# VectorE's order at the group ends and in the drain of a fused convolution and quantised MLP

## The chip, the cores and the metric

One core of a Trainium2 chip runs the whole program. The metric is the time of one execution on the device, in microseconds (us).

## The reference

The input x is 16 images of 192 channels and 32 x 32 pixels, in float32. Two residual blocks follow one another:

```
x = x + dwconv7x7(layernorm_over_channels(x), symmetrised weights)
t = tokens(x)                                   # 16 x 1024 tokens of 192
h = q(layernorm(t) @ sign(W1 - mean).T + b1)    # 768 wide
h = gelu(h, exact)
t = t + q(h @ sign(W2 - mean).T + b2)           # 192 wide
# q, for each of 5 groups of 3 images: gamma = max|y| over the group,
#   clip(y * 128 / (gamma + 1e-5), -128 + 1e-5, 128 - 1e-5); image 16 gives 0
```

The point that shapes the schedule is q: no GELU of a group of images can be computed before the largest absolute value of the group's whole first product is known, and no output before that of the second product.

## The kernel before, in words

Up to about 240 us the program transposes and normalises x, makes the band matrices and does the convolution on TensorE. The change doesn't touch that part. What follows is the token loop, one Python loop `for s in range(-2, FT + LAGF)` written out separately for each engine. The order of the instructions on an engine is the order of this code, and the engines meet only by semaphores. Nothing is rearranged by a planner.

A unit is half an image, 512 tokens. There are FT = 30 units in five groups of GT = 6. Each unit goes through a pipeline over the steps s:

- step u - 2: VectorE normalises four blocks (`normal`, L816), from step 6 on for unit s + 2.
- step u - 1: TensorE turns the tokens round (`tokens`, L1008, L1011), ScalarE and VectorE split them into high and low parts (`token_high`, L546, L548; `token_low`, L822, L824).
- step u: TensorE computes the hidden values in six parts (`hidden`, L1022 to L1024), ScalarE evicts them with the bias (L560).
- step u + 1: VectorE takes the largest absolute value (`largest`, L844). At a group's last unit it also reduces the six values (L847).
- step u + 6 (LAGA): ScalarE's three GELUs (`gelus`, L566). They need the group's scale. In a step with s % 6 == 0 they come at the end of the step.
- step u + 7 (LAGH): the rounding to float16, partly by ScalarE (`high`, L573), partly by VectorE (`high`, L831). Up to unit 22 GpSimd then makes the low parts in six subtractions (L435); from unit 23 (LAST) on VectorE makes half of them itself (L839), GpSimd three.
- step u + 8 (LAG2): TensorE's second product, `lower` (L1054, six pairs of matmuls spread over the step) and `upper` (L1064). The high and low parts lie in two buffers by the unit's parity, so the casts of unit u wait until `upper` of unit u - 2 has ended (`mm2[1]`).
- step u + 9 (LAGE): ScalarE evicts the result (`result`, L584, L587), VectorE takes its largest value (`largest2`, L870, L874).
- step u + 15 (LAGF): the output, `final` (L897, L898): result times scale plus x, where x was turned round by TensorE into two banks of PSUM (`x_back`, L995, L998, L1000) in the step before. TensorE turns x of the next unit into the same banks only when `final` of the last one has ended (`fin`). SyncE stores the output and then fetches x of a later unit from DRAM (`bring_back`), since most of x is parked there.

A group end is a step with s % 6 == 0 from 6 to 30, called `first` in the code. There the scale of the finished group is made: VectorE reduces the six maxima, TensorE transposes them into a row (`as_row`, L1029, on the third part of the step), VectorE reduces the row (`over_row`, L851), TensorE spreads the number to all partitions (`to_all`, L1034, on the fourth part), VectorE computes the scale in five small instructions (`scale`, L856 to L866), and ScalarE's GELUs use it. The row lies in the bank that `final` reads, so TensorE's transpose waits both for the maxima (`gmx`) and for `final` of unit s - 15. TensorE's turning of x on the fifth part of the step waits for the scale. `first2` (s = 15, 21, 27, 33, 39) is the same for the second product (`over_row(1, ..)`, `scale2`).

The drain is the part with s > 30: no hidden products are left, only GELUs (to step 35), casts (to step 36), second products (to step 37) and outputs. The last scale and the last six outputs come in steps 39 to 44.

Of the kernel before, what the change touches and what calls it, by code (L numbers as in the profile page):

```python
# [42 lines left out]
FT = (B // GROUPS * GROUPS) * 2  # L43
# [13 lines left out]
LAGF = LAGE + GT  # L57
# [28 lines left out]
def build(nc, x, cw, w1, b1, w2, b2, out):  # L86
    ctx = ExitStack()
    with ctx:
# [535 lines left out]
        def _(dve):  # L624
# [224 lines left out]
            def over_row(k, g):  # L849
                dve.wait_ge(gtr[k], g)  # L850
                v.tensor_reduce(gs[0:1, k:k + 1], row, AX.X, ALU.max).then_inc(gone[k], 1)  # L851
# [50 lines left out]
            for s in range(-2, FT + LAGF):  # L902
                for k in range(1, len(BATCH)):
                    if BSTEP[k] + 2 == s:
                        scales(k)
                g, g2 = s // GT, (s - LAGF) // GT + 1
                first, first2 = s % GT == 0 and 1 <= g <= FT // GT, (s - LAGF) % GT == 0 and 0 <= s - LAGF < FT
                if first:
                    if 0 <= s - LAGH < FT:
                        high(s - LAGH)  # L910
                    largest(s - 1)
                    if 0 <= s - LAGF < FT:
                        final(s - LAGF)
                    over_row(0, g)
                if s > 5 and s + 2 < FT:
                    normal(s + 2)
                if not first and 0 <= s - LAGH < FT:
                    high(s - LAGH)
                if first2:
                    over_row(1, g2)  # L920
                elif not first and 0 <= s - LAGF < FT:
                    final(s - LAGF)
                if first:
                    scale(g)
                elif 1 <= s <= FT:
                    largest(s - 1)
                if first2:
                    scale2(g2)
                    final(s - LAGF)
                if 0 <= s + 1 < FT:  # L930
                    token_low(s + 1)
                for k in range(len(BATCH)):
                    if BSTEP[k] == s:
                        statistics(k)
                if s == -2:
                    scales(0)
                    normal(0)
                if 0 <= s - LAGE < FT:
                    largest2(s - LAGE)
# [212 lines left out]
```

## Time and profile before

| | |
|---|---|
| median of 3 runs | 635.79 us (635.36 to 638.39) |
| profiled execution, span | 636.4 us |
| TensorE busy | 504.6 us (79%) |
| VectorE busy | 457.2 us (72%) |
| ScalarE busy | 382.7 us (60%) |
| GpSimd busy | 216.1 us (34%) |
| chain that ended last | PE 40%, ACT 23%, DVE 15%, DMA 12%, issue 5% |

The profile comes from one execution of its own, whose span is 0.6 us above the median of the timed runs; no other time is given for it. In the page and the rows PE is TensorE's matmuls, PEld its weight loads, DVE is VectorE, ACT ScalarE, POOL GpSimd, and L844 a line of the kernel. In brackets stands how long the engine was idle before an instruction and what released it. PEclk is the granted clock of TensorE as a share of full speed; its levels are 1.2 and 2.4 GHz. Busy shares are means over stages that have different limits, so each place has to be read for itself.

### The profile page before, as it was taken

What the parts mean: (1) busy time and instruction counts of PE and PEld (TensorE: products, weight loads), DVE (VectorE), ACT (ScalarE), POOL (GpSimd) and SP (SyncE); (2) the same over time, 40 slices, a digit from 0 to 9 for tenths busy, and PEclk for the clock granted to TensorE, in tenths of its full rate; (3) what the DMA queues carried; (4) which work ended last, traced back from release to release, by engine and by line L of the source; (5) the groups of instructions that cost most, each with busy time, mean ns of one, the idle gap of its engine ahead of it and who ended that gap; (6) DMA issues with size and microseconds to landing.
All of it is one profiled execution on the core that took longest, in us unless ns stands there. A gap on an engine that the chain in (4) does not pass through costs nothing.

```text
span 636.4 us, 9847 instructions
## 1 busy us (share of the span) xinstructions
PE 504.6 (79%) x3552; PEld 355.1 (56%) x3552; DVE 457.2 (72%) x1041; ACT 382.7 (60%) x598; POOL 216.1 (34%) x221
## 2 busy tenths in 40 slices
PE   3347348999799987668699899989998999768683
PEld 3346348999799974233345445545564565435452
DVE  7989841222259987977899788897988688665655
ACT  2798920000001355457999799969997798857730
POOL 4000100000300003210486556574848357534430
PEclk9777769999989997789899899989999899979998
DMA  7997225656955639800111001231133333512355
GB/s 221 298 349 205 79 78 165 165 163 172 223 140 142 183 113 396 289 1 1 56 45 51 25 1 41 66 95 49 54 96 101 95 104 100 174 60 90 100 150 173
DMA packets 55280, 81.29 MB, mean 128 GB/s; under 512 B 7361, under 2 KB 39105, under 8 KB 55232
## 3 DMA queue, kind: packets, MB, share of 16 engines
q1 hardware_dynamic: 39616, 68.28, 35.0%
q10 hardware_dynamic: 15136, 11.22, 6.3%
q0 software_dynamic: 480, 1.17, 0.9%
q8 instruction: 28, 0.46, 0.3%
q14 instruction: 20, 0.16, 0.1%
HBM read 53.12 MB, written 27.53 MB: 127 GB/s over the span
## 4 chain that ended last, share of the span: by engine, by line
PE 40%; ACT 23%; DVE 15%; DMA 12%; issue 5%; SPq 3%; ACTq 1%; DVEq 0%
PE bank L972 16%; ACT arena L566 7%; ACT arena L560 6%; DMA arena<-kz_d 5%; PE bank L1054 5%; DMA arena<-x 5%; DVE am L844 5%; PE bank L1064 3%; PE bank L1022 3%; PE bank L1024 2%; PE bank L1023 2%; ACT arena L573 2%; ACT arena L482 2%; PE bank L995 2%; DMA arena<-park_d 2%
## 5 line engine op out<-in xcount | busy, mean ns | idle before, releaser
L435 POOL TENSOR_TENSOR arena<-arena 128x512 f16<-128x512 f32 x159 | 183.2, 1190 | 142.7 <-DVE arena L831 108.6
L560 ACT ACTIVATE arena<-bank,b1s 128x512 f32<-128x512 f32 x180 | 124.7, 703 | 51.7 <-PE bank L1024 51.3
L972 PE MATMUL bank<-arena 128*128 128x112 f32 (+1 forms) x1152 | 135.3, 281 | 21.8 <-ACT arena L482 12.4
L972 PEld LDWEIGHTS bank<-arena 128*128 128x128 f32 x1152 | 133.8, 197 | 22.9 <-ACT arena L482 12.7
L1054 PE MATMUL bank<-arena 128*128 128x512 f16 x360 | 107.7, 394 | 1.7 <-ACT arena L584 1.7
L566 ACT ACTIVATE arena<-arena,gm 128x1024 f32<-128x1024 f32 x90 | 102.7, 1163 | 8.0 <-DVE gm L866 8.0
L844 DVE TENSOR_REDUCE am<-arena 128x1 f32<-128x3072 f32 x30 | 100.3, 3345 | 2.3 <-ACT arena L560 2.3
L750 DVE TENSOR_TENSOR arena<-bank,arena 128x512 f32<-128x512 f32 x48 | 33.2, 692 | 81.2 <-PE bank L972 81.1
L1022 PE MATMUL bank<-arena 128*128 128x512 f16 x180 | 72.0, 400 | 22.6 <-DVE arena L824 11.3
L497 ACT ACTIVATE arena<-arena,wmean 51x576 f16<-51x576 f32 (+1 forms) x10 | 8.6, 856 | 129.2 <-DVE wmean L724 116.4
L1023 PE MATMUL bank<-arena 128*128 128x512 f16 x180 | 71.7, 398 | 0.0
L1024 PE MATMUL bank<-arena 128*128 128x512 f16 x180 | 71.6, 398 | 0.0
L954 PE MATMUL bank<-identf,arena 128*128 128x128 f32 x128 | 34.7, 376 | 38.4 <-DMA arena<-x 38.4
L831 DVE CAST arena<-arena 128x2048 f16<-128x2048 f32 (+1 forms) x30 | 33.0, 1101 | 44.5 <-ACT arena L566 28.2
L1054 PEld LDWEIGHTS bank<-arena 128*128 128x128 f16 x360 | 34.8, 100 | 44.5 <-issue 4.6
L426 POOL TENSOR_SCALAR arena<-arena,VR,SM 128x192 f32<-128x192 f32 x28 | 14.5, 530 | 108.0 <-DVE arena L816 74.9
L1022 PEld LDWEIGHTS bank<-arena 128*128 128x128 f16 x180 | 17.9, 99 | 54.3 <-ACT arena L560 25.3
L816 DVE TENSOR_SCALAR arena<-arena,VR,SM 128x192 f32<-128x192 f32 x92 | 40.5, 501 | 9.4 <-issue 9.0
L1064 PE MATMUL bank<-arena 128*64 128x256 f16 x720 | 46.7, 279 | 0.0
L954 PEld LDWEIGHTS bank<-identf,arena 128*128 128x128 f32 x128 | 23.6, 200 | 39.9 <-DMA arena<-x 29.8
L1064 PEld LDWEIGHTS bank<-arena 128*64 128x64 f16 x720 | 37.9, 110 | 14.2 <-issue 13.6
L573 ACT ACTIVATE arena<-arena 128x1024 f16<-128x1024 f32 x37 | 39.7, 1073 | 5.1 <-PE bank L1064 5.1
(118 smaller groups left out, 684.8 us busy)
## 6 DMA issues: line engine op xcount, KB each, us to landing
arena<-park_d SPq DMA_DIRECT2D x44, 384.0 KB, 3.5
arena<-kz_d SPq DMA_DIRECT2D x100, 112.0 KB, 2.9
arena<-kz_d ACTq DMA_DIRECT2D x92, 112.0 KB, 3.3
park_d<-arena SPq DMA_DIRECT2D x6, 1536.0 KB, 14.5
arena<-x SPq DMA_DIRECT2D x8, 1024.0 KB, 8.9
out<-arena SPq DMA_DIRECT2D x32, 256.0 KB, 2.0
kz_d<-arena SPq DMA_DIRECT2D x8, 672.0 KB, 10.8
arena<-x SPq DMA_DIRECT2D x16, 256.0 KB, 9.4
```

Source lines behind the costliest of these rows:

```text
L435: last = pool.tensor_tensor(out=low_half(u, m, m + 1), in0=yslot(u)[:, 2 * m:2 * m + 2, :], in1=hib(u, m, m + 1), op=ALU.subtract)
L560: act.activation(yslot(s)[:, 2 * m:2 * m + 2, :], m1p[c % 2][:, :].rearrange("p (h n) -> p h n", h=2), ACT.Identity, bias=b1s[:, m:m + 1], ...
L566: act.activation(y, y, ACT.Gelu, scale=gm[:, 5:6]).then_inc(gelu, 1)
L573: last = act.activation(hib(u, m0, m1), yslot(u)[:, 2 * m0:2 * m1, :], ACT.Copy)
L844: v.tensor_reduce(am[:, u % GT:u % GT + 1], yslot(u), AX.XY, ALU.max, apply_absolute_value=True).then_inc(amx, 1)
L954: t.transpose(o[:, b, 0:P], nat[k % 2][:, b, cols], identf[:, :])
L972: last = t.matmul(ps[:, :, lo:hi], WB[BUFS[g]][:, 1 - db, c, :], xn[:, :, lo + db:hi + db], start=(db == 0), stop=(db == -1))
L1022: t.matmul(o, W1A[:, fs], TT[:, s % 2, 0, :], start=True, stop=False)
L1023: t.matmul(o, W1M[:, fs], TT[:, s % 2, 1, :], start=False, stop=False)
L1024: t.matmul(o, W1Q[:, fs], TT[:, s % 2, 2, :], start=False, stop=True).then_inc(mm1, 1)
L1054: last = t.matmul(o, W2T[:, m, 0:P], src, start=(i == n == 0), stop=(i == MT - 1 and n == 1))
L1064: last = t.matmul(m2b[e * C1:(e + 1) * C1, 0:QTR], W2T[:, m, P:C], src[:, e, :], start=(m == n == 0), stop=(m == MT - 1 and n == 1))
```

## The change

Only the order of calls in VectorE's loop changes. No instruction is added or removed on any engine, and the other engines' order is the same as before.

```diff
                 if first:
+                    if 0 <= s - LAGF < FT:
+                        final(s - LAGF)
+                    largest(s - 1)
+                    over_row(0, g)
+                    if s == FT:
+                        scale(g)
                     if 0 <= s - LAGH < FT:
                         high(s - LAGH)
-                    largest(s - 1)
-                    if 0 <= s - LAGF < FT:
-                        final(s - LAGF)
-                    over_row(0, g)
+                    if s < FT:
+                        scale(g)
+                if s > FT and not first2 and 0 <= s - LAGF < FT:
+                    final(s - LAGF)
                 if s > 5 and s + 2 < FT:
                     normal(s + 2)
                 if not first and 0 <= s - LAGH < FT:
                     high(s - LAGH)
                 if first2:
                     over_row(1, g2)
-                elif not first and 0 <= s - LAGF < FT:
+                elif not first and s <= FT and 0 <= s - LAGF < FT:
                     final(s - LAGF)
-                if first:
-                    scale(g)
-                elif 1 <= s <= FT:
+                if not first and 1 <= s <= FT:
                     largest(s - 1)
```

VectorE in step 24, a group end, with a minus where a row stood before and a plus where it stands now. L831 is the cast of unit 17, L844 the largest value of unit 23, L897 the output of unit 9, L816 the normalised blocks of unit 26, L856 and L866 the first and the last instruction of the scale:

```order
-L831 CAST arena<-arena 128x2048 [waits mm2b,gelu]
+L897 SCALAR_TENSOR_TENSOR arena<-arena,gm,bank 128x512 [waits xps]
...
 L844 TENSOR_REDUCE am<-arena 128x1 [waits ev1]
 L847 TENSOR_REDUCE gm<-am 128x1 [waits amx]
-L897 SCALAR_TENSOR_TENSOR arena<-arena,gm,bank 128x512 [waits xps]
...
 L851 TENSOR_REDUCE gs<-bank 1x1 [waits gtr0]
-L816 TENSOR_SCALAR arena<-arena,VR,SM 128x192 [waits trQ,ld_l2,nm]
...
+L831 CAST arena<-arena 128x2048 [waits mm2b,gelu]
 L856 TENSOR_SCALAR gm<-bank 128x1 [waits gall]
...
 L866 TENSOR_SCALAR gm<-gm 128x1 [waits gelu,gsc_t]
+L816 TENSOR_SCALAR arena<-arena,VR,SM 128x192 [waits trQ,ld_l2,nm]
```

The output moved ahead of the largest value, the cast behind the row's reduction, and the four blocks behind the scale. In steps 6 and 12 there is no output unit, and in step 6 no cast.

VectorE in step 30 before, from the cast of unit 23 to the result's largest value:

```order
L831 CAST arena<-arena 128x1024 [waits mm2b,gelu]
L839 TENSOR_TENSOR arena<-arena 128x1024 [waits hiV]
L839 TENSOR_TENSOR arena<-arena 128x512 [waits hiA]
L844 TENSOR_REDUCE am<-arena 128x1 [waits ev1]
L847 TENSOR_REDUCE gm<-am 128x1 [waits amx]
L897 SCALAR_TENSOR_TENSOR arena<-arena,gm,bank 128x512 [waits xps]
L898 SCALAR_TENSOR_TENSOR arena<-arena,gm,bank 128x256
L851 TENSOR_REDUCE gs<-bank 1x1 [waits gtr0]
L856 TENSOR_SCALAR gm<-bank 128x1 [waits gall]
...
L866 TENSOR_SCALAR gm<-gm 128x1 [waits gelu,gsc_t]
L870 TENSOR_REDUCE am<-arena 128x1 [waits ev2]
```

The same stretch now:

```order
L897 SCALAR_TENSOR_TENSOR arena<-arena,gm,bank 128x512 [waits xps]
L898 SCALAR_TENSOR_TENSOR arena<-arena,gm,bank 128x256
L844 TENSOR_REDUCE am<-arena 128x1 [waits ev1]
L847 TENSOR_REDUCE gm<-am 128x1 [waits amx]
L851 TENSOR_REDUCE gs<-bank 1x1 [waits gtr0]
L856 TENSOR_SCALAR gm<-bank 128x1 [waits gall]
...
L866 TENSOR_SCALAR gm<-gm 128x1 [waits gelu,gsc_t]
L831 CAST arena<-arena 128x1024 [waits mm2b,gelu]
L839 TENSOR_TENSOR arena<-arena 128x1024 [waits hiV]
L839 TENSOR_TENSOR arena<-arena 128x512 [waits hiA]
L870 TENSOR_REDUCE am<-arena 128x1 [waits ev2]
```

The cast and the two subtractions moved behind the scale, the output to the front.

VectorE in a step of the drain (31, 32, 34, 35, 36), here step 34, with minus and plus as above:

```order
+L897 SCALAR_TENSOR_TENSOR arena<-arena,gm,bank 128x512 [waits xps]
+L898 SCALAR_TENSOR_TENSOR arena<-arena,gm,bank 128x256
 L831 CAST arena<-arena 128x1024 [waits mm2b,gelu]
 L839 TENSOR_TENSOR arena<-arena 128x1024 [waits hiV]
 L839 TENSOR_TENSOR arena<-arena 128x512 [waits hiA]
-L897 SCALAR_TENSOR_TENSOR arena<-arena,gm,bank 128x512 [waits xps]
-L898 SCALAR_TENSOR_TENSOR arena<-arena,gm,bank 128x256
```

The output, which waits only for x to be turned round in the step before, moved ahead of the cast, which waits for the second product.

## Rows read from the trace of the kernel before

**Rows 1.** Stretches: us; busy PE, PEld, DVE, ACT, POOL; PEclk, DMA share, GB/s
```profile
484.00:500.00 16.00, 13.29 (x74) 7.31 (x73) 12.36 (x22) 8.23 (x13) 6.76 (x6) 0.79 0.24 75
500.00:510.00 10.00, 9.37 (x60) 5.17 (x62) 7.43 (x7) 10.00 (x15) 6.16 (x6) 1.00 0.33 85
```

**Rows 2.** Chain of work that ended last, step 24: start, us, what
```profile
484.89 1.23 DVE arena L831
486.12 3.27 DVE am L844
...
489.57 0.66 DVE arena L897
490.23 0.40 DVE arena L898
```

**Rows 3.** Timeline, steps 24 and 25: start, us, engine, line, operation, idle before and releaser
```profile
482.28 0.93 DVE L870 TENSOR_REDUCE am<-arena 128x1 f32<-128x768 f32 x1
482.53 0.71 ACT L560 ACTIVATE arena<-bank,b1s 128x512 f32<-128x512 f32 x1
...
486.19 6.76 POOL L435 TENSOR_TENSOR arena<-arena 128x512 f16<-128x512 f32 x6 [2.62 <-DVE arena L831]
...
490.72 0.37 PE L1029 MATMUL bank<-identf,gm 128*1 128x128 f32 x1 [2.71 <-DVE arena L898]
...
491.34 2.30 DVE L816 TENSOR_SCALAR arena<-arena,VR,SM 128x192 f32<-128x192 f32 x4
...
494.43 0.21 DVE L866 TENSOR_SCALAR gm<-gm 128x1 f32<-128x1 f32 x1
...
496.92 1.25 DVE L816 TENSOR_SCALAR arena<-arena,VR,SM 128x192 f32<-128x192 f32 x4
```

**Rows 4.** Timeline, step 12 (first row) and step 18 (the two others)
```profile
358.79 0.27 PE L1029 MATMUL bank<-identf,gm 128*1 128x128 f32 x1 [2.10 <-DVE gm L847]
...
418.33 1.23 DVE L831 CAST arena<-arena 128x2048 f16<-128x2048 f32 x1 [0.35 <-ACT arena L566]
...
424.16 0.27 PE L1029 MATMUL bank<-identf,gm 128*1 128x128 f32 x1 [2.67 <-DVE arena L898]
```

**Rows 5.** Timeline, step 30, the last group end
```profile
549.29 0.95 DVE L870 TENSOR_REDUCE am<-arena 128x1 f32<-128x768 f32 x1
...
552.75 0.69 DVE L831 CAST arena<-arena 128x1024 f16<-128x1024 f32 x1 [2.51 <-ACT arena L566]
...
560.45 0.37 PE L1029 MATMUL bank<-identf,gm 128*1 128x128 f32 x1 [6.93 <-DVE arena L898]
...
563.13 3.23 ACT L566 ACTIVATE arena<-arena,gm 128x1024 f32<-128x1024 f32 x3 [8.02 <-DVE gm L866]
```

**Rows 6.** Timeline, steps 35 to 37
```profile
599.61 2.38 PE L1054 MATMUL bank<-arena 128*128 128x512 f16 x10
599.78 1.06 ACT L573 ACTIVATE arena<-arena 128x1024 f16<-128x1024 f32 x1 [0.77 <-PE bank L1064]
599.79 0.69 DVE L831 CAST arena<-arena 128x1024 f16<-128x1024 f32 x1 [2.31 <-PE bank L1064]
...
602.04 3.22 ACT L566 ACTIVATE arena<-arena,gm 128x1024 f32<-128x1024 f32 x3
...
602.22 3.93 POOL L435 TENSOR_TENSOR arena<-arena 128x512 f16<-128x512 f32 x3 [3.40 <-ACT arena L573]
...
604.04 0.63 PE L995 MATMUL bank<-identf,arena 128*128 128x128 f32 x4 [2.06 <-issue]
...
605.48 1.53 PE L1064 MATMUL bank<-arena 128*64 128x256 f16 x24
...
605.65 0.69 ACT L584 ACTIVATE arena<-bank,b2s 128x512 f32<-128x512 f32 x1 [0.39 <-PE bank L1054]
...
617.72 0.63 PE L995 MATMUL bank<-identf,arena 128*128 128x128 f32 x4 [1.09 <-DMA arena<-park_d]
```

**Rows 7.** DMA issues of the page: size, median us from issue to landing
```profile
arena<-park_d SPq DMA_DIRECT2D x44, 384.0 KB, 3.5
```

## The prediction

> **What bounds the kernel now.** I read the chain of waits first, from step 6 of the token loop on, then the timeline of all engines at each group end (steps 12, 18, 24, 30) and in the drain (steps 31 to 38), then the stretches. A step in the middle of a group takes about 10 us and belongs to ScalarE, which is busy all 10.00 us of such a stretch while TensorE is busy 9.37 [rows 1]; nothing in it changes. The places that change are those where ScalarE isn't the bound.
>
> At a group end the chain goes through VectorE: cast of the step, largest value, then the output of one unit, and only then TensorE turns the maxima into a row [rows 2]. TensorE stands idle before that transpose for 2.10, 2.67, 2.71 and 6.93 us in steps 12, 18, 24 and 30 [rows 3 to 5]. The cast of step 24 itself begins late: VectorE is free at 482.28 + 0.93 = 483.2 us and starts it at 484.9, because it waits for the last GELU; the last eviction that the largest value needs has ended by 482.53 + 0.71 = 483.2. After the transpose, four normalised blocks (2.30 us) stand ahead of the scale, which ends at 494.6 [rows 3]. In this stretch TensorE's granted clock averages 0.79, so part of it is at the lower level (1.2 GHz) after that idle time [rows 1].
>
> In the drain there is a loop across three engines: the last products of a unit end, VectorE casts at 599.8, makes low parts, then writes the output, and only then TensorE's turning of the next unit's x starts at 604.0, after 2.06 us in which it is idle [rows 6]. It has five of six product pairs behind it and the sixth and the upper products (1.53 us) still ahead, and these release the next cast. One round is 7.3 us, from the cast at 599.78 to the end of the next upper products at 605.48 + 1.53 = 607.0, which release the next cast at 607.1. In step 30 ScalarE waits 8.02 us for the scale [rows 5].
>
> **Steps 12, 18 and 24.** The number of instructions is the same; the order of VectorE alone moves. In step 24 the new order is: final output from 483.2, 0.66 + 0.40 = 1.06 us [rows 2], to 484.3; largest value 3.3 us to 487.6, the small reduction 0.2, so that the maxima can be turned at 487.9 and not at 490.7. That is 2.8 us, and TensorE has 2.71 us of idle time there to give: 2.7. In step 12 there is no output unit; the reduction starts when its eviction is done and no longer behind a cast that waited for its GELUs, and the gain is TensorE's whole idle time, 2.1. In step 18 the cast hardly waited, so that only its 1.2 us and a wait of 0.35 go: 1.5 of the 2.67 [rows 4]. Sum 6.3.
>
> The scale comes earlier still, since the four blocks no longer precede it, but on the path that only removes what TensorE waits for it in front of turning x, and makes the clock's fall less likely. If 0.79 became 1.00 over 16 us, 3.4 us would go [rows 1]; if the clock stays as it is, 0. I take 1.3 for step 24, the part on the path between, and 0.8 and 0.9 for steps 18 and 12: 3.0 together. Group ends before the last: 6.3 + 3.0 = 9.3 us, bounds 4 and 14. ScalarE's GELUs, which begin when the step's evictions are done, carry the gain to the next step, since ScalarE is the bound there.
>
> What is made later: the cast of step 24 starts at about 488.6 and not at 484.9, so GpSimd's six subtractions (6.76 us, 1.13 each [rows 3]) end at 496.7 and not 493.0, and in step 18 they start 5.0 us later, in step 12 3.3. The first product of the next step wants four of them: about 494.5 in step 24. With the gain TensorE comes to that product at about 496.4, 1.9 us after. In steps 12 and 18 I find 1.5 and 1.1 us of slack in the same way. So this costs nothing, narrowly. The four blocks now stand behind the scale and delay the low parts of the next tokens: in step 6, where nothing else moves, by 0.85 us, which lies beside ScalarE's three GELUs of 3.2 us; it costs nothing either. If that cover were gone, 0.85 in each of four steps, 3.4 in all.
>
> A row and a page differ on the price of those blocks. The row has four blocks in 2.30 us while GpSimd is at its subtractions [rows 3]; the next four, at 496.92 with GpSimd idle, take 1.25. The Trainium skill (SBUF — State Buffer, "SBUF: two separate sides") says that the two engines share a port pair under an exclusive lock, so that a VectorE instruction in a two-port mode is fully blocked while GpSimd's runs. By the page alone each of the four could wait for a whole subtraction. That would be 4 x 1.13 = 4.5 us more, against the 1.05 us that the row shows, and the tokens' low parts would come 3.4 us later in each of three steps, beyond the slack: 10 us back and a time of 622. I go by the row.
>
> **Step 30.** Now: the cast waits until 552.75, its two low parts follow, then largest value, output, transpose at 560.45, scale, GELUs at 563.13 [rows 5]. New: VectorE is free at 549.29 + 0.95 = 550.2, output to 551.4, largest value to 554.7, transpose 555.0, row, broadcast, scale at 557.2, GELUs at 557.4. The cast and low parts (some 2.8 us) come after the scale, at 557.3 to 560.1, and the products that read them come at about 561.4. Gain 5.7 us. Bounds: 6.9, the idle time of TensorE, and 4.0 if the cast, now 4.6 us later, holds the first product of step 31.
>
> **The drain.** The output goes ahead of the casts in steps 31, 32, 34, 35, 36; in step 33, which ends a group for the second scale, it doesn't.
> - Step 31: TensorE no longer waits 2.06 us for the output, as long as in step 35 [rows 6], and the clock there is partly low, so the upper products end 3.7 us earlier; ScalarE, which turns to its next cast only after three GELUs and a result, follows by 2.4. Step 32 carries two more turnings of x and is TensorE's own; it lets 3.4 through until step 33.
> - Step 33: 0.
> - Steps 34 and 35: without the output TensorE needs about 2.1 us for five pairs (the row of 2.38 us, its end modelled) and 607.0 - 604.0 = 3.0 for the rest: 5.1. ScalarE needs from its cast at 599.78 to the end of the GELUs at 605.26, then 0.69 for a result and a little between: 6.25 us [rows 6]. That is the new bound, against 7.3: 1.05 each, 2.1.
> - Steps 36 and 37: the last unit's cast is then at H, GpSimd's three subtractions end 6.4 after it (602.22 + 3.93 - 599.78 [rows 6]), and two pairs and the 3.0 follow: 10.2 us from cast to the end of the upper products, against 13.5 now (607.1 to 620.6), where TensorE waited for an output in step 36 and for a parked block in step 37 (idle 1.09 [rows 6]). 3.3.
> Sum of step 30 and drain: 5.7 + 3.4 + 2.1 + 3.3 = 14.5. Low bound 8 (half of the drain's part lost), high 17.
>
> The 15.8 us behind the last upper products (one scale, six outputs, their stores) stay.
>
> **Sum.** 9.3 + 14.5 = 23.8 us, against a span of 636.4 in the profiled execution, which is 0.6 above the median of 635.79. I subtract from the median and keep half a microsecond for edges that I can't see: 635.8 - 23.3 = 612.5. This is a long sum of terms that all point one way, so the range leans upwards.
>
> **Rivals.**
> A. The group ends give nothing back to the step after: the casts are late, the products of the next step wait for GpSimd, and the 9.3 go. For: slack of 1 to 2 us only. Against: before the change the same subtractions were done many microseconds ahead. 635.8 - 14.5 = 621.3.
> B. In the drain the parked x becomes the bound. Each block is fetched only after an output two units before, with 3.5 us from issue to landing [rows 7] and about 1.6 us of other issues in front. For: step 37 already waits for it [rows 6]. Against: 5.1 + 1.2 + 1.3 is under 8 us, and it has two steps of 6.25. If half of the drain's 8.8 goes: 617.
> C. Slower: late casts decide. In steps 12, 18 and 24 the subtractions come 3.3, 5.0 and 3.7 us later and in step 30 the cast 4.6; if the following product waited all of that, and no group end gained, 16.6 us would be added, and the drain's 8.8 taken off: 643.6. It decides from the point where TensorE reaches the next step's first product before the fourth subtraction; the rows say that it comes 1 to 2 us after.
> D. The path is unmoved, because another wait of the same length stands behind each: 635.8. The 6.93 us of idle TensorE with ScalarE idle for 8.02 at once speaks against it [rows 5].
>
> **How the numbers follow.** My case 0.68 (own range 608 to 618), A 0.11, B 0.13, C 0.04, D 0.04. About 0.5% (3.2 us) is what a measurement can tell from no change. Faster: 0.68 + 0.11 + 0.13 and a little of D's spread = 0.93; same 0.03; slower 0.04. The range takes my case, B and most of A: 608 to 622.
>
> **What would show it.** In the profile after: TensorE's idle time before the transpose of the maxima gone in steps 12 and 24, 1.1 us or so left in step 18, under 4 in step 30; the three GELUs of step 30 starting 5.7 us earlier relative to its start; in steps 34 to 36 upper products 6.2 to 6.3 us apart and no TensorE idle time in front of turning x; clock above 0.9 in step 24. I am wrong if product matmuls wait for GpSimd's subtractions after a group end, if x turned in the drain waits for a DMA, or if the upper products stay 7.3 us apart.

## The result, and the profile after

| | before | after |
|---|---|---|
| median | 636.62 us (635.36 to 638.39, 4 runs) | 617.99 us (612.76 to 620.0, 4 runs) |
| ratio | | 0.9708, 95% interval 0.9664 to 0.9752 |
| span of the profiled execution | 636.4 us | 615.9 us (its time 617.74) |
| TensorE, VectorE busy | 504.6, 457.2 us | 496.8, 467.1 us |
| chain that ended last | PE 40%, ACT 23%, DVE 15% | PE 42%, DVE 22%, ACT 18% |

The change is worth 18.6 us between medians. 612.5 had been forecast, with 608 to 622 around it. VectorE, whose instructions are the same in number and kind, is busy for 10 us more: some of them take longer than before. The chain now goes through VectorE for 22% of the span. The page's list of the lines on the chain now has two that its list before did not have, VectorE's L816 and L831:

```profile
PE bank L976 19%; DMA arena<-x 6%; PE bank L1058 5%; ACT arena L566 5%; DVE am L844 5%; ACT arena L560 4%; DMA arena<-kz_d 3%; PE bank L1026 3%; PE bank L1027 3%; PE bank L1028 3%; PE bank L1068 2%; DVE arena L816 2%; DVE arena L831 2%; ACT
```

L816, the normalised blocks, and L831, the cast, have 2% each. VectorE's lines below 900 keep their numbers; TensorE's are four higher (L1029 became L1033, L1064 became L1068, L1054 became L1058, L1022 became L1026, L995 became L999).

**The group ends.** Timeline of steps 12 and 13 (one row each), 18 and 19 (one row each), 24 and 25, as in [rows 3] and [rows 4]:

```profile
357.65 0.27 PE L1033 MATMUL bank<-identf,gm 128*1 128x128 f32 x1
...
365.50 0.61 PE L1026 MATMUL bank<-arena 128*128 128x512 f16 x1 [2.44 <-DVE arena L824]
...
422.47 0.27 PE L1033 MATMUL bank<-identf,gm 128*1 128x128 f32 x1 [0.81 <-DVE gm L847]
...
430.32 0.39 PE L1026 MATMUL bank<-arena 128*128 128x512 f16 x1 [1.57 <-DVE arena L824]
...
481.47 3.34 DVE L844 TENSOR_REDUCE am<-arena 128x1 f32<-128x3072 f32 x1
...
485.25 0.27 PE L1033 MATMUL bank<-identf,gm 128*1 128x128 f32 x1
...
485.77 1.20 DVE L831 CAST arena<-arena 128x2048 f16<-128x2048 f32 x1
...
487.05 6.82 POOL L435 TENSOR_TENSOR arena<-arena 128x512 f16<-128x512 f32 x6 [6.19 <-DVE arena L831]
...
487.74 3.99 DVE L816 TENSOR_SCALAR arena<-arena,VR,SM 128x192 f32<-128x192 f32 x4
...
492.36 0.68 DVE L824 TENSOR_TENSOR arena<-bank,arena 64x512 f16<-64x512 f32 x1
493.10 0.39 PE L1026 MATMUL bank<-arena 128*128 128x512 f16 x1 [1.57 <-DVE arena L824]
...
493.83 1.23 DVE L816 TENSOR_SCALAR arena<-arena,VR,SM 128x192 f32<-128x192 f32 x4
```

The transpose of the maxima (L1033) waits for nothing in steps 12 and 24 and 0.81 us in step 18, where it had waited 2.10, 2.71 and 2.67. So far it went as forecast. But four normalised blocks, now behind the scale, take 3.99 us beside GpSimd's subtractions, where the same four take 1.23 us later with GpSimd idle. Behind them stand the low parts of the next tokens (L822, L824), and TensorE's first hidden product of the next step (L1026) waits for these: 2.44, 1.57 and 1.57 us. The chain of waits from step 12 into step 13 says the same. Its columns are start, us, what:

```profile
360.14 3.99 DVE arena L816 x4
364.12 0.61 DVE arena L822
...
364.76 0.69 DVE arena L824
...
365.50 0.61 PE bank L1026
```

**Step 30 and the drain**, timeline of steps 30 to 35, as in [rows 5] and [rows 6]:

```profile
546.89 0.27 PE L1033 MATMUL bank<-identf,gm 128*1 128x128 f32 x1 [1.36 <-DVE gm L847]
...
548.74 1.28 DVE L831 CAST arena<-arena 128x1024 f16<-128x1024 f32 x1
548.85 3.23 ACT L566 ACTIVATE arena<-arena,gm 128x1024 f32<-128x1024 f32 x3 [1.73 <-DVE gm L866]
...
553.02 2.37 PE L1058 MATMUL bank<-arena 128*128 128x512 f16 x10 [1.16 <-DVE arena L839]
...
554.99 5.21 POOL L435 TENSOR_TENSOR arena<-arena 128x512 f16<-128x512 f32 x3 [3.95 <-ACT arena L573]
...
555.39 3.82 DVE L839 TENSOR_TENSOR arena<-arena 128x1024 f16<-128x1024 f32 x2
...
561.01 1.64 DVE L831 CAST arena<-arena 128x1024 f16<-128x1024 f32 x1
...
566.46 0.69 DVE L831 CAST arena<-arena 128x1024 f16<-128x1024 f32 x1
...
567.18 2.91 DVE L839 TENSOR_TENSOR arena<-arena 128x1024 f16<-128x1024 f32 x2
...
567.57 4.62 POOL L435 TENSOR_TENSOR arena<-arena 128x512 f16<-128x512 f32 x3 [1.07 <-ACT arena L573]
...
570.31 0.58 PE L1038 MATMUL bank<-gs,arena 1*128 1x1 f32 x2 [3.01 <-DVE gs L851]
```

In step 30 TensorE's 6.93 us of idle time are 1.36 and ScalarE's 8.02 are 1.73. In the steps after it VectorE's cast and its two low parts (L839) run at the same time as GpSimd's three, and both get longer: 3.82 us for two low parts and 5.21 for GpSimd's three. In step 33, the group end of the second product, TensorE waits 3.01 us for the row's reduction (L851), which stands behind cast and low parts. It waited 2.36 us there before.

**Step by step.** The table gives the time from one unit's upper products to the next (L1064 before, L1068 after); "start" is the first of them (step 8), "loop" the time from there to the last. The last three kernels are experiments told below. Steps not shown are within 0.1 us of each other, step 27 apart (12.01 to 12.47).

```
step    before  after  drain_only early_ends_only last_end_only
start   322.05 323.16  320.47     320.89          320.73
12       13.91   9.97   13.83       9.97           12.22
13        9.85  12.94    9.93      13.14            9.93
18       14.81  11.33   14.80      11.69           14.81
19       10.81  11.48   10.81      11.47           10.81
24       16.22  10.37   14.34      10.37           14.34
25       10.81  11.47   10.81      11.47           10.80
30       15.08   7.77   15.33      15.32            7.76
31        8.07   6.29    5.54       8.30           10.79
32        8.19   6.87    6.88       7.33            7.38
33        8.91  12.56    9.69       8.89           10.05
34        7.33   5.39    5.07       7.33            7.94
35        7.33   6.29    6.29       7.32            8.31
36        7.31   5.94    5.94       7.31            7.31
37        6.36   5.08    5.08       6.08            5.59
loop    297.10 275.60  286.26     287.78          290.36
```

The span is 20.5 us shorter: 21.5 in the loop, -1.1 at its start, 0.1 behind. Four rows went against the change: step 13 (+3.1), steps 19 and 25 (+0.7 each) and step 33 (+3.65).

Two things about comparing single executions. The start varies by 8 us between the kernels here (316.8 to 324.8), though up to there the code differs only in the group end of step 6, and that moves little: from VectorE's largest value of unit 5, in step 6, to the start it takes 25.7 us before and 25.6 after. And a step's time depends on the granted clock of that execution: step 24 with the same code took 16.22 us before, at 0.79, and 14.34 in drain_only and last_end_only, at 1.00; step 12 took 13.91 before, at 0.88, and 12.22 in last_end_only, at 1.00. So some 3.6 us of the 21.5 are the clock of the one profiled execution before. Stretches of the profile after, steps 12, 13, 30 and 33 (columns as in [rows 1]):

```profile
351.56:361.53 9.97, 9.65 (x67) 5.21 (x66) 7.72 (x12) 9.11 (x15) 4.22 (x4) 1.00 0.00 0
361.53:374.47 12.94, 10.50 (x63) 5.32 (x62) 12.15 (x15) 10.24 (x15) 10.53 (x11) 0.87 0.11 32
542.57:550.34 7.77, 5.99 (x50) 3.40 (x49) 6.67 (x12) 6.01 (x8) 4.48 (x5) 1.00 1.00 350
563.50:576.06 12.56, 8.59 (x48) 4.71 (x48) 10.16 (x18) 6.53 (x8) 7.62 (x5) 0.75 0.23 67
```

And of the kernel before, steps 12, 30 and 33:

```profile
350.44:364.35 13.91, 11.49 (x67) 5.60 (x67) 10.50 (x16) 9.30 (x15) 8.91 (x8) 0.88 0.07 13
...
550.57:565.65 15.08, 8.15 (x48) 4.42 (x47) 9.10 (x14) 7.03 (x9) 5.24 (x5) 0.77 0.53 180
581.91:590.82 8.91, 5.87 (x48) 3.44 (x47) 5.67 (x12) 6.17 (x7) 4.59 (x4) 1.00 0.30 89
```

The clock (the column 0.88, 0.77, 1.00) changed in both directions: it is full now in steps 12 and 30, where TensorE's idle time before the transpose went from 2.10 us to none and from 6.93 to 1.36, and lower in step 13 and in step 33, behind idle times of 2.44 and 3.01 us. In step 12 that is not shown to be the change's doing, since last_end_only had a full clock there with the old order and the same 2.10 us.

### The profile page after: what moved, and what is told of

Same layout as the page of the kernel before. It is cut to its first block, busy times and chain, and to the rows that moved or that the text cites. A ratio compares the mean times of both kernels' runs of the same rounds, so it can differ in the third digit from the quotient of the medians.

```text
span 615.9 us, 9847 instructions
## 1 busy us (share of the span) xinstructions
PE 496.8 (81%) x3552; PEld 353.5 (57%) x3552; DVE 467.1 (76%) x1041; ACT 382.0 (62%) x598; POOL 219.7 (36%) x221
## 4 chain that ended last, share of the span: by engine, by line
PE 42%; DVE 22%; ACT 18%; DMA 10%; issue 5%; SPq 3%; ACTq 0%; DVEq 0%
PE bank L976 19%; DMA arena<-x 6%; PE bank L1058 5%; ACT arena L566 5%; DVE am L844 5%; ACT arena L560 4%; DMA arena<-kz_d 3%; PE bank L1026 3%; PE bank L1027 3%; PE bank L1028 3%; PE bank L1068 2%; DVE arena L816 2%; DVE arena L831 2%; ACT arena L482 2%; DVE arena L766 2%
## 5 line engine op out<-in xcount | busy, mean ns | idle before, releaser
L435 POOL TENSOR_TENSOR arena<-arena 128x512 f16<-128x512 f32 x159 | 186.9, 1212 | 120.6 <-DVE arena L831 99.3
L1058 PE MATMUL bank<-arena 128*128 128x512 f16 x360 | 106.4, 390 | 5.4 <-ACT arena L584 3.6
L844 DVE TENSOR_REDUCE am<-arena 128x1 f32<-128x3072 f32 x30 | 100.3, 3343 | 3.5 <-ACT arena L560 3.5
L1026 PE MATMUL bank<-arena 128*128 128x512 f16 x180 | 71.0, 395 | 26.0 <-DVE arena L824 17.7
L1027 PE MATMUL bank<-arena 128*128 128x512 f16 x180 | 70.6, 392 | 0.0
L1028 PE MATMUL bank<-arena 128*128 128x512 f16 x180 | 70.2, 390 | 0.0
L958 PE MATMUL bank<-identf,arena 128*128 128x128 f32 x128 | 33.4, 365 | 40.9 <-DMA arena<-x 40.9
L1058 PEld LDWEIGHTS bank<-arena 128*128 128x128 f16 x360 | 34.5, 99 | 47.7 <-issue 4.6
L816 DVE TENSOR_SCALAR arena<-arena,VR,SM 128x192 f32<-128x192 f32 x92 | 44.1, 539 | 8.4 <-issue 8.2
L1026 PEld LDWEIGHTS bank<-arena 128*128 128x128 f16 x180 | 17.8, 99 | 56.6 <-DVE arena L824 21.3
L831 DVE CAST arena<-arena 128x2048 f16<-128x2048 f32 (+1 forms) x30 | 35.8, 1195 | 13.6 <-ACT arena L566 11.9
L1068 PE MATMUL bank<-arena 128*64 128x256 f16 x720 | 46.1, 276 | 0.0
L1068 PEld LDWEIGHTS bank<-arena 128*64 128x64 f16 x720 | 37.5, 109 | 13.8 <-issue 13.4
```

The lines of the kernel that those rows point to most:

```text
L435: last = pool.tensor_tensor(out=low_half(u, m, m + 1), in0=yslot(u)[:, 2 * m:2 * m + 2, :], in1=hib(u, m, m + 1), op=ALU.subtract)
L816: last = v.tensor_scalar(TN[:, h % 2, jj, :], x1[:, jj, :], VR[:, n:n + 1], SM[:, n:n + 1], ALU.mult, ALU.add)
L844: v.tensor_reduce(am[:, u % GT:u % GT + 1], yslot(u), AX.XY, ALU.max, apply_absolute_value=True).then_inc(amx, 1)
L958: t.transpose(o[:, b, 0:P], nat[k % 2][:, b, cols], identf[:, :])
L1026: t.matmul(o, W1A[:, fs], TT[:, s % 2, 0, :], start=True, stop=False)
L1027: t.matmul(o, W1M[:, fs], TT[:, s % 2, 1, :], start=False, stop=False)
```

## The experiments

The medians of before that stand beside them are 634.62 us (632.2 to 638.49, 12 runs) for drain_only, early_ends_only, last_end_only and blocks_last, 635.12 (7 runs) for the two less_gpsimd kernels and 634.82 (11 runs) for the others. Every ratio is to before.

**The parts of the change.** The theory: the parts add up. The rival: they take from each other, since they share VectorE and GpSimd. drain_only moves only the output in steps 31 to 36:

```diff
+                if s > FT and not first2 and 0 <= s - LAGF < FT:
+                    final(s - LAGF)
...
-                elif not first and 0 <= s - LAGF < FT:
+                elif not first and s <= FT and 0 <= s - LAGF < FT:
```

> The kernel before with the drain's part of the change alone (output first in steps 31, 32, 34, 35, 36). My sum (terms independent, step 30 apart): 8.8 us less, about 627.5, upper products of steps 34 to 36 about 6.0 to 6.3 us apart. The rival, read from the changed kernel's trace, where step 33 took 12.6 us instead of 8.9: the drain's part gives its steps back in step 33, so only 4 to 6 us less, 631 to 632.

625.92 us, ratio 0.9835 (0.9799 to 0.987). Steps 31 to 37 together take 44.49 us and not 53.50, which is 9.0 for a forecast of 8.8. The step's period with the output in front is 6.29 in step 35, against 6.25 worked out: the drain's part was right. In it the low parts of VectorE take 1.37 + 0.76 us and GpSimd's three 3.94 in step 31: nothing overlaps.

early_ends_only has the new order in steps 6 to 24 and the old one in step 30 and the drain:

```diff
-                if first:
+                if first and s < FT:
+                    if 0 <= s - LAGF < FT:
+                        final(s - LAGF)
+                    largest(s - 1)
+                    over_row(0, g)
+                    if 0 <= s - LAGH < FT:
+                        high(s - LAGH)
+                    scale(g)
+                if first and s == FT:
```

> The kernel before with the new order in steps 6, 12, 18 and 24 alone. If the group ends' gains add up as in the changed kernel's trace (0.9 + 2.8 + 5.4): 9 us less, about 627.5. My sum had 9.3. Rival A (the late casts give it all back): 636.5, no change, and product matmuls waiting for GpSimd in steps 13, 19 and 25.

629.21 us, 0.9918 (0.988 to 0.9957): 5.2 us off by the ratio, where 9 were expected and none by rival A. The table has the longer steps 13, 19 and 25 as in the whole change. Its loop is 9.3 shorter than before's in the profiles, but before's profiled execution had the lower clock in steps 12 and 24. Against last_end_only, which has the old order there at a full clock in both, steps 12, 13, 18, 19, 24 and 25 are together 4.8 us shorter (68.11 and 72.91).

last_end_only has the new order in step 30 alone:

```diff
+                if first and s == FT:
+                    final(s - LAGF)
+                    largest(s - 1)
+                    over_row(0, g)
+                    scale(g)
+                    high(s - LAGH)
```

> The kernel before with the new order in step 30 alone. My sum: 5.7 us less, about 631. If the cast that now comes after the scale holds back step 31 (TensorE idle for 1.16 us there in the changed kernel) and nothing else follows from it: 5 to 7 less. If step 33 is lengthened by whatever makes the steps before it shorter: 2 to 4 less, 633.

631.83 us, 0.9921 (0.9889 to 0.9952): 5.0 us off by the ratio, 2.8 between the medians. Step 30 gave 7.3 us, and steps 31 to 37 took 57.37 and so 3.9 back. In the timeline of step 31 the output stands behind cast and low parts that are late, and TensorE's turning of x behind the output:

```profile
557.74 2.93 DVE L839 TENSOR_TENSOR arena<-arena 128x1024 f16<-128x1024 f32 x2
...
558.37 4.40 POOL L435 TENSOR_TENSOR arena<-arena 128x512 f16<-128x512 f32 x3 [3.95 <-ACT arena L573]
...
561.79 1.09 PE L1001 MATMUL bank<-identf,arena 128*128 128x128 f32 x4 [3.00 <-issue]
```

The idle 3.00 us and the doubled transposes (1.09 against 0.60) make this step 10.79. The loops of the three parts are 10.8, 9.3 and 6.7 us shorter, 26.9 in all, and that of the whole is 21.5. That looks as if the parts took from each other, but they don't. In steps 12, 13, 18, 19, 24 and 25 drain_only and last_end_only have the code of before, and 1.9 and 3.5 us of their gain lie there: the low clock of before's execution is counted once for each part. Where each part changes something, early_ends_only gives 8.3 us (in these six steps, 76.41 to 68.11), drain_only 8.8 and last_end_only 3.5 (steps 30 to 37, 68.58 to 59.82 and to 65.13). That is 20.5 in all, and the whole gives 21.2 in the same steps (8.9 and 12.4). So the parts add up, and no row shows the rival. The new step 30 costs the drain 3.9 us with either order of the output (57.37 against 53.50; 48.42 in the change against 44.49). The timed runs are too coarse to decide it: by the ratios the parts are 10.5, 5.2 and 5.0 us, 20.7 together, between the medians 16.9, and the change is 18.6.

**The normalised blocks.** Theory: their delay in steps 13, 19 and 25 goes if they stand behind the tokens' low parts, which read PSUM. Rival: the lateness lies with GpSimd. blocks_last, on the changed kernel:

```diff
-                if s > 5 and s + 2 < FT:
+                if s > 5 and s + 2 < FT and not first:
                     normal(s + 2)
...
                     token_low(s + 1)
+                if first and s + 2 < FT:
+                    normal(s + 2)
```

> The changed kernel with the four normalised blocks of steps 6, 12, 18 and 24 moved further back, behind the next tokens' low parts. If the blocks, which took 3.99 us beside GpSimd's subtractions, are what holds the next step's first product (TensorE idle there for 2.44, 1.57 and 1.57 us, and the clock low in step 13): 3 to 4.5 us less than the changed kernel, about 614. If ScalarE is the bound there all the same, as I had predicted: the same time, 618.

608.99 us, 0.9574 (0.9523 to 0.9625), an interval that lies wholly below that of the change. Steps 13, 19 and 25 are 9.93, 10.81 and 10.80, as before, 4.35 us less than in the change, and step 18 is 10.36, 1.0 less. The loop is 268.90, 6.7 less; 1.5 of that is step 33, whose code is the change's. The 9.0 us between the medians are more than the 3 to 4.5 expected, but only the 4.35 are shown to be the blocks'. Timeline of step 12:

```profile
356.51 6.83 POOL L435 TENSOR_TENSOR arena<-arena 128x512 f16<-128x512 f32 x6 [5.74 <-DVE arena L831]
...
357.20 0.68 DVE L822 TENSOR_TENSOR arena<-bank,arena 128x512 f16<-128x512 f32 x1
...
358.52 3.79 DVE L816 TENSOR_SCALAR arena<-arena,VR,SM 128x192 f32<-128x192 f32 x4
...
361.12 0.61 PE L1060 MATMUL bank<-arena 128*128 128x512 f16 x2 [0.25 <-POOL arena L435]
```

The blocks are still slow (3.79) but nothing on the path waits for them. L822 beside GpSimd takes its usual 0.68. The first pair of the second product in step 13 now does wait for GpSimd, 0.25 us: the mechanism of the prediction's rival A begins here. In steps 19 and 25 it waits for nothing.

gpsimd_after_blocks takes the overlap away from the other side. In the three steps GpSimd starts its subtractions only when the blocks are done:

```diff
                 pool.wait_ge(hiV, u + 1)
+                if u in (5, 11, 17):
+                    pool.wait_ge(tnv, u + 10)
```

> The changed kernel in which GpSimd's subtractions of units 5, 11 and 17 start only when VectorE's four normalised blocks of steps 12, 18 and 24 are done. If the blocks are long (3.99 us) because GpSimd works at the same time: 1.25 us here, the tokens' low parts 2.7 us earlier, and in steps 13, 19 and 25 the first product waits for GpSimd instead, since the fourth subtraction then ends about 2 us later than now; each of these steps within 1 us of the changed kernel's. If they are long for another reason: 3.99 us still and the steps 2 us longer.

One execution: 611.67 us, span 609.8, a loop of 274.04. Timeline of steps 12 and 13:

```profile
355.52 1.24 DVE L818 TENSOR_SCALAR arena<-arena,VR,SM 128x192 f32<-128x192 f32 x4
...
356.91 6.81 POOL L435 TENSOR_TENSOR arena<-arena 128x512 f16<-128x512 f32 x6 [7.82 <-DVE arena L818]
...
358.86 3.84 DVE L818 TENSOR_SCALAR arena<-arena,VR,SM 128x192 f32<-128x192 f32 x4
...
361.52 1.03 PE L1060 MATMUL bank<-arena 128*128 128x512 f16 x2 [2.32 <-POOL arena L435]
```

The same four blocks take 1.24 us without GpSimd beside them. That shows the cause of the 3.99. But the time doesn't go: the next four meet the subtractions instead (3.84), TensorE waits 2.32 us for GpSimd, and step 13 is 13.06. The late GpSimd is as dear as the late blocks.

**Step 33.** Theory: cast and low parts ahead of the row's reduction cost the 3.65 us. casts_after_33 puts them behind the output in that step:

```diff
-                if not first and 0 <= s - LAGH < FT:
+                if not first and s != FT + 3 and 0 <= s - LAGH < FT:
...
                     final(s - LAGF)
+                    if s == FT + 3:
+                        high(s - LAGH)
```

> The changed kernel with the casts and low parts of step 33 behind the second scale and the output. Step 33 took 12.56 us in the changed kernel against 8.91 before. If it is VectorE's cast chain (begun 1.3 us late, 0.5 longer beside GpSimd) that stands between the second product's maxima and its scale, and the low clock follows from TensorE's idle time: step 33 at 8 us or less, the casts cost at most 1 us in step 34, time 4 to 5 us below the changed kernel. If step 33 is bound by another thing (ScalarE, a fetch of parked x): 12 us still, no change.

611.18 us, 0.9618 (0.9569 to 0.9666), 6.8 us below the change between the medians. Step 33 is 9.28, where 8 or less was expected. That is 3.3 less than in the change, but 1.7 less than the 11.02 of blocks_last, which has the change's code from step 30 on and the same steps 30 to 32 to 0.01 us. The steps behind it don't give it back (34 to 37: 5.08, 6.28, 5.95, 5.08). 1.5 us more of its loop of 270.86 are the clock in step 13 (11.48).

The other theory of step 33 is that VectorE is late because its instructions and GpSimd's meet. less_gpsimd_after leaves GpSimd one low part of three in units 23 to 29. The two others are left out altogether, and TensorE reads the high part twice in their place, so that its work stays the same and the result is not the reference's:

```diff
-                low(u, 0, LP)
+                low(u, LP - 1, LP)
...
-                return hib(u, m, m + 1), low_half(u, m, m + 1)
+                return hib(u, m, m + 1), (hib if u >= LAST and m < LP - 1 else low_half)(u, m, m + 1)
```

> The changed kernel in which GpSimd makes one of its three subtractions for units 23 to 29 (two low parts of the second product's input are left out, the products take the high part twice in their place). If the overlap with GpSimd is what lengthens VectorE's cast and low parts in the drain (3.82 us for the two low parts of step 31, 2.8 in step 32, against 2.1 alone) and so step 33: the low parts back to 2.1 to 2.4 us, step 33 under 11.5 instead of 12.56. If VectorE's delay comes from the order alone: 12.5 still.

One execution: 609.12 us, span 607.3, a loop of 273.35. Timeline of steps 31 and 33:

```profile
548.63 1.35 DVE L839 TENSOR_TENSOR arena<-arena 128x1024 f16<-128x1024 f32 x1
...
550.29 0.75 DVE L839 TENSOR_TENSOR arena<-arena 128x512 f16<-128x512 f32 x1 [0.30 <-ACT arena L573]
...
563.14 0.38 PE L1038 MATMUL bank<-gs,arena 1*128 1x1 f32 x2 [2.03 <-DVE gs L851]
```

The low parts are back to 1.35 + 0.75 us, step 31 is 5.28 and step 33 is 9.67, 2.9 less than in the change, without any change of VectorE's order.

But these 2.9 us can't be put down to GpSimd. From step 30 on blocks_last and gpsimd_after_blocks have the code of the change too. Their steps 33, columns as above:

```profile
555.58:566.60 11.02, 8.58 (x48) 4.71 (x48) 8.62 (x17) 6.53 (x8) 6.60 (x5) 0.71 0.21 68
...
560.48:570.21 9.73, 7.40 (x49) 4.32 (x49) 6.41 (x14) 7.11 (x9) 6.22 (x6) 0.82 0.11 37
```

With GpSimd's full work the same code gives 12.56, 11.02 and 9.73 us. VectorE's low parts in steps 30 to 33 take 12.4, 11.6 and 9.6 us together in these three and 8.3 in less_gpsimd_after. So step 33 is shorter where the two engines meet less, but how much they meet differs from one execution to the next, and what the overlap alone costs in step 33 stays open. Steps 30 to 33 together take 33.5, 32.0 and 31.1 us, and 30.9 in less_gpsimd_after.

less_gpsimd_before is the same edit on the kernel before, as a control:

> The same omission in the kernel before, as the control. There the casts and GpSimd's subtractions hardly overlap in the drain and GpSimd ends long before its parts are read: every step of the drain within 0.1 us of what it was (step 33 at 8.9).

One execution: 634.03 us, span 632.2, a loop of 296.48 against 297.10. The expectation was missed step by step: 33, 34 and 35 took 10.09, 7.86 and 8.37. The stretches of 33 and 34:

```profile
575.97:586.06 10.09, 7.14 (x48) 4.21 (x47) 5.66 (x12) 6.17 (x7) 1.68 (x1) 0.83 0.33 93
586.06:593.92 7.86, 5.79 (x45) 3.23 (x44) 4.67 (x6) 6.17 (x7) 1.69 (x1) 0.92 0.28 94
```

VectorE is busy for 5.66 us and ScalarE for 6.17, as before in its step 33 (5.67 and 6.17, above); only the clock, 0.83 and not 1.00, and with it TensorE's 7.14 us for 5.87, are different. So taking GpSimd's work off gains VectorE nothing where the two don't meet. It also shows that a step like 33 can differ by over 1 us between executions by its clock, and that the 9.67 and 9.28 above have at least such an uncertainty.

**Step 30's cast.** cast_before_scale_30 keeps the change but puts the cast and low parts of step 30 ahead of the scale. It asks what that place is worth:

```diff
                     over_row(0, g)
-                    if s == FT:
-                        scale(g)
                     if 0 <= s - LAGH < FT:
                         high(s - LAGH)
-                    if s < FT:
-                        scale(g)
+                    scale(g)
```

> The changed kernel with the cast and the two subtractions of step 30 ahead of the scale again, as in the other group ends. My step: the scale, and with it ScalarE's GELUs, comes some 2.2 us later, the wait of 1.16 us in step 31 for the low parts goes: 1 to 2 us slower. Rival: the cast beside GpSimd is what lengthens the drain, so putting it earlier gains: 1 to 3 us faster.

619.87 us, 0.9753 (0.9704 to 0.9801): 1.9 us above the change, of the 1 to 2 expected, though the two intervals overlap. Timeline of step 30:

```profile
546.72 4.88 POOL L435 TENSOR_TENSOR arena<-arena 128x512 f16<-128x512 f32 x3 [3.28 <-ACT arena L573]
...
548.46 3.73 DVE L839 TENSOR_TENSOR arena<-arena 128x1024 f16<-128x1024 f32 x2
...
552.97 3.23 ACT L566 ACTIVATE arena<-arena,gm 128x1024 f32<-128x1024 f32 x3 [6.33 <-DVE gm L866]
```

Step 30 is 13.64, 5.9 more than in the change, where 2.2 had been expected: the low parts beside GpSimd are 3.73 and not 2.1 us, and TensorE idles for 5.02 and then turns x at the lower clock. But the cast of step 31 no longer meets GpSimd's three, step 33 is 8.89 (12.56 in the change), and so only 3.2 of the 5.9 are left in the loop (278.80).

**Both mends together.** best is blocks_last with the cast of step 33 behind its output:

> Both mends together: the normalised blocks of steps 6 to 24 behind the tokens' low parts, and step 33's casts behind the output. If the two are independent: blocks_last (0.957 of the kernel before) less 3 to 5 us, about 605, a ratio of 0.950.

608.66 us (607.37 to 611.88, 7 runs), 0.9579 (0.9539 to 0.9619), and 605 had been expected. It beats the kernel before and the change, but not blocks_last. Step 33 is 7.63, the shortest of all, and the loop 267.84, the shortest too. But that is 1.1 below blocks_last (268.90), whose step 33 was 11.02: steps 18, 27, 34 and 37 are 0.5 to 1.3 longer. What makes these longer I did not settle. Nor is it settled why the second mend, worth 6.8 us between the medians on the change alone, is worth 0.3 on top of blocks_last.

```
step    after  blocks_last casts_after_33 cast_before_30 gpsimd_after_blocks best   less_gpsimd_after
start   323.16  320.24      320.45         322.27         318.55             324.82  316.82
12        9.97    9.96        9.97           9.97           9.96               9.97    9.96
13       12.94    9.93       11.48          12.98          13.06               9.93   12.97
18       11.33   10.36       11.53          11.22          11.32              11.63   11.84
27       12.04   11.88       12.04          12.52          13.16              12.38   12.30
30        7.77    7.76        7.76          13.64           8.84               7.75    9.05
33       12.56   11.02        9.28           8.89           9.73               7.63    9.67
34        5.39    5.23        5.08           6.60           5.08               5.88    5.05
37        5.08    5.08        5.08           5.08           5.08               5.64    5.05
loop    275.60  268.90      270.86         278.80         274.04             267.84  273.35
```

## Why the prediction was right, and where it was not

| step | forecast | measured, profiled executions |
|---|---|---|
| 12 and 13 | -3.0 | -0.9; against the full clock of last_end_only +0.8 |
| 18 and 19 | -2.3 | -2.8 |
| 24 and 25 | -4.0 | -5.2, of which 1.9 are the lower clock of before's execution |
| 30 | -5.7 | -7.3 |
| 31 and 32 | -3.4 | -3.1 |
| 33 | 0 | +3.7 |
| 34 and 35 | -2.1 | -3.0 |
| 36 and 37 | -3.3 | -2.7 |
| other steps of the loop | 0 | -0.3 |
| start, tail | 0 | +1.1, -0.1 |
| sum | -23.8 | -20.5 |

Each row is rounded by itself. Part of the agreement is luck: against the forecast 7.8 us went missing (2.1 in steps 12 and 13, 3.7 in step 33, 1.1 at the start, the rest in steps 31, 32, 36 and 37) and some 4.5 came on top.

**What held.** The direction, the places and most sizes. The transpose's idle time went in steps 12 and 24, and 0.81 us of it stayed in step 18 (1.1 forecast). Step 35 became ScalarE's at 6.29 us (6.25 forecast); steps 34 and 36, forecast alike, took 5.39 and 5.94. The parked x bounds nothing in the drain (rival B), and nothing came out slower (rival C).

**"It costs nothing either": the four blocks.** This step failed. The prediction took the blocks' delay of the next tokens' low parts, 0.85 us, from step 6, where they take 1.23 us and GpSimd has no subtractions yet, set it beside ScalarE's GELUs, and priced the overlap with GpSimd by a row in which the four took 2.30 us [rows 3]. But TensorE, not ScalarE, needs those low parts first, and in their new place the blocks always lie wholly within GpSimd's six subtractions: 3.99 us. They cost 3.1, 0.7 and 0.7 us in steps 13, 19 and 25, 4.4 together, and in step 13 the clock fell (0.87). blocks_last got these back, in the profiles to within 0.1 us of before's steps. In that price I had read a row of partial overlap as the price of full overlap. Of rows 3 themselves, GpSimd's six ran from 486.19 to 492.95 and the blocks from 491.34 to 493.64: only 1.6 of their 2.30 us lay beside it. The trace of before had a nearer row, in step 12, where 2.7 us lay beside the six and the blocks took 3.13:

```profile
355.11 3.35 DVE L844 TENSOR_REDUCE am<-arena 128x1 f32<-128x3072 f32 x1
...
355.27 6.77 POOL L435 TENSOR_TENSOR arena<-arena 128x512 f16<-128x512 f32 x6 [2.69 <-DVE arena L831]
...
359.31 3.13 DVE L816 TENSOR_SCALAR arena<-arena,VR,SM 128x192 f32<-128x192 f32 x4
```

The Trainium skill (SBUF — State Buffer, "SBUF: two separate sides") has this pair of ports as an exclusive lock, and the prediction set its rule aside for the row. The trace agrees that the two hinder each other, but not by a whole subtraction for each block: the blocks lose 3.99 - 1.23 = 2.8 us, midway between the row's 1.05 and the 4.5 estimated from the page. The time of 622 worked out from that estimate did not come, since it took 3.4 us in each of three steps and two of them lost 0.7.

**"Step 33: 0."** This failed too, and by 3.65 us it is the largest error of the sum. Before, its cast began 1.65 us after the upper products of the step before (581.91 to 583.56), and TensorE waited 2.36 us for the row's reduction. After, the cast begins 2.96 us after them (563.50 to 566.46): +1.3. From cast to row it is 3.54 and not 3.02: +0.5. From row to output 0.2. The rest, 1.6, lies between the output and the upper products, which TensorE does at the lower clock after 3.01 us of idle time. What the prediction had wrong is that cast and low parts stay ahead of the second scale's row there and arrive late: with them behind the output, step 33 takes 9.28 (casts_after_33). That they are late goes with the same meeting of the two engines: with cast and low parts 4 to 4.6 us later in step 30, counted from its start, while GpSimd's three start as they did (4.6 us after it), VectorE's work of steps 30 to 32 lies on GpSimd's. How much of the 3.65 us that alone costs isn't shown, since the same code gave 9.73 to 12.56.

**Step 30 was undersized** by 1.6 us. The order gave what was worked out, TensorE's idle 6.93 going to 1.36 (5.6), and the clock, 0.77 in this step before and 1.00 now, gave the rest; I had counted the clock at the other group ends and not here. Steps 34 and 35 gave 0.9 more: 35 went as forecast, and 34, which follows the late step 33, is 5.39.

**The base of the sum.** The profile's 636.4 is a span. In every run whose time is given beside it the time is 1.8 to 1.9 us longer, so that by this estimate this execution took about 638.2, at the upper end of before's runs (638.39) and not 0.6 above their median. From its own time the forecast sum gives 614.4, and the execution after took 617.74. Setting the sum against the median counted as gain a clock that was low in this one execution.

**Rival A** (GpSimd's late subtractions take the group ends' gain) decided nothing in the change, where the late blocks hide it; its wait is 0.25 us in blocks_last and 2.32 in gpsimd_after_blocks. Its direction was right: the slack, read as 1.1 to 1.9 us, was about 0.5 in steps 19 and 25 of blocks_last and none in step 13.

## What to carry to other kernels

When an order moves VectorE's work to another time, look at what GpSimd does at that time, and price each moved instruction from a row in which the two overlap wholly, not in part. The subtractions with one input in PSUM kept their 0.68 us there, so they should come first, and SBUF-to-SBUF work behind them. When a change is taken apart, compare each part in the steps that it touches: a low clock in the one baseline execution is otherwise counted once for every part. Take a sum of durations from one execution against that execution's own time, clock included; and after a gain at one place, follow the next period-setting loop to see where the same two engines meet next.

## What was unexpected of the hardware

- Four 128x192 float32 TENSOR_SCALAR on VectorE take 1.23 us alone and 3.79 to 3.99 beside GpSimd's 128x512 subtractions. GpSimd isn't slowed by them (6.82 us for six, 6.75 to 6.78 before).
- VectorE's subtractions, with two inputs in SBUF, and GpSimd's slow each other: 3.82 for 2.1 us, and 5.21 to 5.56 for 3.93 in steps 31 and 32. A cast of 128x1024 took 1.28 to 1.64 for 0.69.
- VectorE's low parts from PSUM stay at 0.68 us with GpSimd busy beside them. The largest value over 128x3072 takes 3.35 us beside GpSimd (355.11 in before) and 3.34 with GpSimd idle (481.47).
- Most steps repeat to 0.01 us between executions where the clock is full (step 12 is 9.96 or 9.97 in eight kernels). Step 27 doesn't: 11.88 to 13.16 us at a clock of 1.00. In the profiled executions the rest of the spread is the start (316.8 to 324.8 us), the clock after an idle time (step 24: 16.22 or 14.34 with the same code) and step 33 (9.73 to 12.56 with the same code).
